# A Mamba scan on four engines: the table of slots in which TensorE, ScalarE and GpSimd do the side work, rewritten

## The reference, cut to what matters

```python
mu = seq.mean(-1, keepdims=True)
var = ((seq - mu) ** 2).mean(-1, keepdims=True)
h = (seq - mu) * jax.lax.rsqrt(var + EPS) * ln_g + ln_b
xz = h @ in_w
xs, z = jnp.split(xz, 2, axis=-1)             # 192 + 192 channels
xc = silu(depthwise causal conv of xs, 4 taps, + conv_b)
dbl = xc @ xproj_w
dt, Bm, Cm = split(dbl)                        # 6, 16, 16
delta = jax.nn.softplus(dt @ dt_w + dt_b)
dA = jnp.exp(delta[..., None] * A)             # 192 channels x 16 states
dBx = delta[..., None] * Bm[:, :, None, :] * xc[..., None]
hstates = scan: h_t = dA_t * h_(t-1) + dBx_t
y = jnp.einsum('blds,bls->bld', hstates, Cm) + Dp * xc
y = y * jax.nn.silu(z)
return seq + y @ out_w
```

## Time and profile before

| what | value |
|---|---|
| median of 3 runs | 7506.49 us |
| the profiled execution's own time | 7508.82 us |
| its span in the trace | 7506.7 us |
| TensorE, matmul busy | 6068.7 us (81%) |
| VectorE busy | 6432.9 us (86%) |
| ScalarE busy | 5446.9 us (73%) |
| GpSimd busy | 5465.7 us (73%) |
| Mamba phase | from 0 to about 2844 us |

### The profile page before, as it was taken

One profiled execution on the slowest core, in us unless ns is written; L12 is line 12 of the kernel. 1 busy time (PEld: TensorE's weight loads), 2 busy tenths in 40 slices (PEclk: granted clock), 3 DMA queues, 4 the chain that ended last, 5 costly groups with the idle time before them and its releaser, 6 DMA issues. The chain is left out here.

```text
span 7506.7 us, 105881 instructions
## 1 busy us (share of the span) xinstructions
PE 6068.7 (81%) x18336; PEld 2113.4 (28%) x18336; DVE 6432.9 (86%) x7490; ACT 5446.9 (73%) x11128; POOL 5465.7 (73%) x4289
## 2 busy tenths in 40 slices
PE   7888888888888872888888888888887768798696
PEld 2222222222222220222222222222222113498252
DVE  6999999999999995499999999999999985533636
ACT  7888888888888873577777778777777764322757
POOL 5888888888888881488898898888888871000606
PEclk8999999889989986888999999999999888997898
DMA  4445445445445445587888888888877773346222
GB/s 101 108 104 117 107 106 116 107 108 115 106 106 116 106 101 143 115 186 182 186 187 185 187 189 186 185 188 187 187 183 186 184 165 92 124 137 195 81 57 77
DMA packets 584349, 1050.60 MB, mean 140 GB/s; under 512 B 105735, under 2 KB 140732, under 8 KB 579100
## 3 DMA queue, kind: packets, MB, share of 16 engines
q1 hardware_dynamic: 584060, 1047.70, 58.7%
HBM read 857.89 MB, written 189.54 MB: 140 GB/s over the span
## 5 line engine op out<-in xcount | busy, mean ns | idle before, releaser
L1644 POOL TENSOR_TENSOR scan_prod<-scan_hs,scan_BC_rep 128x512 f32<-128x512 f32 x1536 | 1943.8, 1273 | 312.8 <-DVE scan_hs L1568 303.8
L664 POOL TENSOR_TENSOR mamba_prod<-mamba_hs,mamba_BC_rep 128x512 f32<-128x512 f32 x1536 | 1919.7, 1274 | 216.6 <-DVE mamba_hs L621 214.8
L621 DVE TENSOR_TENSOR_SCAN mamba_hs<-mamba_dA,mamba_carry,mamba_dbx 128x512 f32<-128x512 f32 x1152 | 1425.3, 1265 | 1.6
L1193 PE MATMUL scan_u_rep<-scan_du,scan_sel 96*128 96x512 f32 x1536 | 935.2, 693 | 538.7 <-DVE scan_hs L1568 538.5
L546 ACT ACTIVATE mamba_dA<-mamba_delta_rep,mamba_a_neg 128x512 f32<-128x512 f32 x1536 | 1092.5, 712 | 121.5 <-DVE mamba_hs L621 118.8
L1418 ACT ACTIVATE scan_dA<-scan_delta_rep,scan_a_neg 128x512 f32<-128x512 f32 x1536 | 1092.3, 712 | 96.1 <-DVE scan_hs L1568 84.7
L1568 DVE TENSOR_TENSOR_SCAN scan_hs<-scan_dA,scan_carry,scan_dbx_even 128x512 f32<-128x512 f32 x768 | 975.8, 1271 | 45.6 <-ACT scan_carry L1398 27.9
L1568 DVE TENSOR_TENSOR_SCAN scan_hs<-scan_dA,scan_carry,scan_u_rep 128x512 f32<-128x512 f32 x768 | 976.3, 1271 | 40.8 <-ACT scan_carry L1398 36.7
L600 DVE TENSOR_TENSOR mamba_dbx<-mamba_u_rep,mamba_BC_rep 128x512 f32<-128x512 f32 x1152 | 776.7, 674 | 88.1 <-PE mamba_u_rep L332 75.6
L1967 POOL TENSOR_TENSOR ffn_sq<-ffn_xm 96x512 f32<-96x512 f32 x64 | 66.3, 1036 | 954.4 <-DVE ffn_xm L1935 943.3
L332 PE MATMUL mamba_u_rep<-mamba_du,mamba_sel 96*128 96x512 f32 x768 | 466.5, 692 | 317.4 <-DVE mamba_hs L621 316.9
(11 more groups left out here) (286 smaller groups left out, 10776.8 us busy)
## 6 DMA issues: line engine op xcount, KB each, us to landing
scan_BC_rep<-proj_rows SPq DMA_DIRECT2D x1024, 256.0 KB, 6.4
scan_delta_rep<-proj_rows SPq DMA_DIRECT2D x1024, 192.0 KB, 3.6
mamba_BC_rep<-bc_units SPq DMA_DIRECT2D x512, 256.0 KB, 8.1
mamba_delta_rep<-delta_units SPq DMA_DIRECT2D x512, 192.0 KB, 3.7
proj_rows<-scan_dbc SPq DMA_DIRECT2D x256, 224.0 KB, 3.4
delta_units<-mamba_delta SPq DMA_DIRECT2D x128, 192.0 KB, 5.8
by_n<-fin_res SPq DMA_DIRECT2D x32, 768.0 KB, 3.2
fmid_src<-by_n SPq DMA_DIRECT2D x32, 768.0 KB, 5.2
```

The lines of the kernel that those rows point to most:

```text
L621: nc.vector.tensor_tensor_scan(hs[:, s % RING_H], dA[:, s % RING_A], dbx_bank(s)[:], carry[:, bass.ds(at, 1)], op0=ALU.mult, op1=ALU.add). ...
L664: pool.tensor_tensor(prod[:, (G * u + s) % RING_P], hs[:, s % RING_H], BC_rep[:, u, QUADS + s % QUADS], ALU.mult).then_inc(s_prod, 1)
L1193: nc.tensor.matmul(u_rep[c][:], sel[:, c], du[:, k], start=True, stop=True).then_inc(s_rep_u, 1)
L1644: pool.tensor_tensor(prod[:, (G * k + s) % RING_P], hs[:, (G * k + s) % RING_H], BC_rep[:, k, 2 + s % 2], ALU.mult).then_inc(s_prod, 1)
```

## The change

Only the numbers of slots change, and with them the order of instructions on TensorE, ScalarE and GpSimd. VectorE's and SyncE's code stays as it is. No instruction is added or taken away from a slot's work. (The changed file is three lines shorter, so its line numbers are 1 to 3 lower.)

TensorE, `next_step`, `ahead_step` and the output product:

```diff
-                if s == 0:
+                if s == 1:
                     project_z(lay, m, 1)
-                elif s == 3:
-                    project(lay, m, v, 0)
-                elif s == 5:
-                    project(lay, m, v, 1)
+                elif s == 4:
+                    for half in range(2):
+                        project(lay, m, v, half)
...
-                if s == 8:
+                if s == 10:
                     mean(m, v)
-                elif s == 10:
+                elif s == 12:
                     var(m, v)
...
-                    if s == 9 and prev is not None:
+                    if s == 7 and prev is not None:
                         project_out(prev, n - 1, 1 - u, 0)
                         project_out(prev, n - 1, 1 - u, 1)
```

ScalarE:

```diff
-                if s in (3, 4, 6):
-                    to_raw(lay, m, {3: 1, 4: 2, 6: 3}[s])
-                elif s == 5:
+                if s in (4, 7, 8):
+                    to_raw(lay, m, {4: 1, 7: 2, 8: 3}[s])
+                elif s == 6:
                     silu_x(m, v)
-                elif s == 9:
+                elif s == 12:
                     softplus_begin(lay, m, 0)
                     softplus_end(m, 0)
-                elif s == 11:
+                elif s == 14:
                     copy_bc(m)
                     softplus_begin(lay, m, 1)
-                elif s == 12:
                     softplus_end(m, 1)
-                elif s == 14:
                     silu_z(m, v)
```

More of the change, by code:

```diff
@@ L507, in next_step @@
             def next_step(s, lay, m, v):
-                if s in (3, 4, 6):
-                    to_raw(lay, m, {3: 1, 4: 2, 6: 3}[s])
-                elif s == 5:
+                if s in (4, 7, 8):
+                    to_raw(lay, m, {4: 1, 7: 2, 8: 3}[s])
+                elif s == 6:
                     silu_x(m, v)
-                elif s == 9:
+                elif s == 12:
                     softplus_begin(lay, m, 0)
                     softplus_end(m, 0)
-                elif s == 11:
+                elif s == 14:
                     copy_bc(m)
                     softplus_begin(lay, m, 1)
-                elif s == 12:
                     softplus_end(m, 1)
-                elif s == 14:
                     silu_z(m, v)
             def ahead_step(s, lay, m):
-                if s == 13:
+                if s == 15:
                     square(m)
-                elif s == 16:
+                elif s == 17:
                     rsqrt(m)
@@ L529, in ahead_step @@
                     affine(lay, m)
-                elif s == 23:
+                elif s == 22:
                     to_raw(lay, m, 0)
@@ L555, in body @@
                         next_step(s, nxt, n + 1, 1 - u)
-                    if s == 10 and prev is not None:
+                    if s == 8 and prev is not None:
                         evict_y(n - 1, 1)
-                    if s == 20:
+                    if s == 19:
                         evict_y(n, 0)
-                    if s == 15 and prev is not None:
+                    if s == 19 and prev is not None:
                         evict_out(n - 1)
@@ L665, in body @@
                                        ALU.mult).then_inc(s_prod, 1)
-                    if s == 6 and prev is not None:
+                    if s == 5 and prev is not None:
                         gate(n - 1, 1 - u, 1)
-                    if s == 18:
+                    if s == 20:
                         gate(n, u, 0)
@@ L675, in ahead_step @@
             def ahead_step(s, m):
-                if s == 12:
+                if s == 14:
                     normalise(m)
             def next_step(s, m, v):
-                if s == 5:
+                if s == 8:
                     add_softplus(m, v, 0)
-                elif s == 8:
+                elif s == 12:
                     add_softplus(m, v, 1)
-                elif s == 9:
+                elif s == 15:
                     input_times_delta(m, v)
```

## The result

The changed kernel takes 7539.44 us (median of 6 runs, 7536.70 to 7542.45) against 7504.63 us for the kernel before (6 runs, 7494.86 to 7511.48). The ratio is 1.0047, with an interval of 1.0034 to 1.0059: **slower by 35 us** where I had forecast 26 us faster (7480 against 7506.49). The profiled execution took 7542.45 us with a span of 7540.3, 33.6 us more than before.

What follows compares the result with a forecast made beforehand. VectorE, 98.5% busy in the Mamba phase, was taken as the bound, with 26.8 us of waits for TensorE to gain. 7508.8 - 29.9 + 3.2 = 7482.1, less 2.3 for the profiled run, gave 7480 us, range 7470 to 7500.

Steps and rivals of the forecast that it cites:

- SyncE: DMA-issuing queue, same code: B and C go some 3 us later, later transfers wanted only next unit; cost nothing.
- second kind of waits: VectorE's 24 waits, 12.4 us, put down to its own scans where the two-unit loop body starts again; left as is.
- TensorE, slots 7 to 12: Mamba units: slot 11's `rep_input` starts early enough, margin 1.1 to 3.8 us; gain 29.9 us, bounds 0 and 29.9.
- 34 waits: VectorE's waits for TensorE's `rep_input` before the `dbx` of group 16, 26.8 us in all; claimed to go.
- TensorE, slots 0 to 4: Mamba units: both projections in slot 4 start at the same moment as before, the last z product later; nothing.
- ScalarE, slot 14: Mamba units: eight instructions in one piece take 6.84 us; `dA` of slot 15 ready with margin 2.4 us; nothing.
- GpSimd: Mamba units: `du` moves to slot 15 behind `normalise`, ends at 32.6 us into the unit, wanted at 34.9; nothing.
- Prologue: Before the units: projection starts about 1.2 us later and 2.02 us of `var` stand bare; cost 3.2 us, bounds 0 and 6.
- Sum: Whole kernel: 7508.8 - 29.9 + 3.2 = 7482.1, predicted as 7480 us, 0.35% less.
- The third: Rival: VectorE waits for `du` or spreads of B and C at a unit's group 0; 0.5 us each, 7511; chance 0.06.
- The first: Rival: ScalarE too late with `dA` for scan 15, 3.0 us in some 62 units, 7666 us; chance 0.10.
- The second: Rival: TensorE still late in slot 11, half the waits at group 16 come back, 7495 us; chance 0.14.

Runs made afterwards that it cites:

- burst at 26: Changed kernel with SyncE holding the unit's second burst of transfers until scan 1 of the next unit is done; 7488.11 us, ratio 0.9967 to the kernel before.

## Why the prediction was wrong

**The step that failed** is SyncE: "Its code is the same but what it waits for shifts [...] Nothing." It is tied to the sentence on the second kind of waits, "No edit touches VectorE's code, so I leave it as it is." I had the shift right. It gave the store of `delta` half 0 at about T0 + 18 (18.0 in unit 19 after) and B and C some 3 us later than T0 + 19.0 (21.9). Then I asked only whether the data would be there when it is wanted, and for the later transfers wrote "wanted in the next unit". That holds: no wait for a DMA appeared. But I didn't lay out the second burst, and didn't ask what else uses the DMA engines at T0 + 42. In SyncE's order the store of `delta` half 1 stands behind the reads of B and C (issued at 912.65 before, 931.76 after), and the burst waits about 10 us until that store has landed (941.86 - 931.76 = 10.1 after, 922.96 - 912.65 = 10.3 before). So it shifts with B and C, from T0 + 32.1 to 37.1, and its transfers last to about T0 + 43. The 24 waits at the turn were listed, and I took their 0.5 us for a fixed price. By the runs that price isn't fixed: it depends on what the DMA engines are doing at the turn. This term was +54 us where I had put 0, and taken out (burst at 26) it leaves 7488.

**The other steps, in the order of the text.**

- *TensorE, slots 7 to 12*: right. `copy_bc` starts at T0 + 16.5 (16.6 laid out), `mean` at 18.4 (18.4 laid out), the `rep_input` of slot 11 at 21.3 (21.2 at full clock), `var` at 25.1 (about 25.0). All 34 waits went. TensorE's granted clock from 66 to 2830 us rose from 0.90 to 0.93.
- *TensorE, slots 0 to 4*: right, ScalarE's 63 waits for the first projection (153.2 us) are gone.
- *ScalarE, slot 14*: right. From `copy_bc` at 921.22 to the `dA` of slot 15 at 927.96 the block takes 6.74 us (6.84), and VectorE never waits for `dA`. Each table load is followed by its ACTIVATE after 1.30 us. With 2.66 us per switch, the rule of the Trainium skill (ScalarE: Activation LUTs, What ACT_TABLE_LOAD costs), the block would by my estimate have been about 9.5 us; this case's trace doesn't agree with that rule, and the measurement decides.

```profile
921.22 0.59 ACT L487 ACTIVATE mamba_bc<-mamba_pre 32x512 f32<-32x512 f32 x1
...
924.29 1.28 ACT L465 ACT_TABLE_LOAD   x1
925.59 1.06 ACT L465 ACTIVATE mamba_xz<-mamba_raw 96x1024 f32<-96x1024 f32 x1
926.66 1.28 ACT L466 ACT_TABLE_LOAD   x1
927.96 0.72 ACT L543 ACTIVATE mamba_dA<-mamba_delta_rep,mamba_a_neg 128x512 f32<-128x512 f32 x1
```

- *GpSimd*: right. `xh` starts at T0 + 27.7 (27.7), and `du` ends at 32.6 (32.6).
- *Prologue*: mechanism right, size just over its upper bound: +6.3 against 3.2, bounds 0 and 6. The projection started 1.1 us later (1.2), but took 7.04 us instead of 5.37 at a lower clock:

```profile
36.55 7.04 PE L317 MATMUL mamba_pre<-mamba_xz,mamba_w_proj 96*96 96x512 f32 x8 [3.26 <-ACT mamba_raw L453]
```

  The granted clock of that stretch, 36 to 44 us, is 0.57, and was 0.72 over 35 to 41 us before. It isn't the same in each run: with the burst at 26, whose prologue is the same code, the same eight products took 5.34 us and the first `dbx` was at 69.72, +3.8. So in part this size was bad luck.
- *Sum*: with the turns as they were, the forecast was 7480 from a kernel at 7506.49, 0.35% less; measured with the burst at 26, 0.33% less. "First `dbx` near 69 us and last scan near 2807": that kernel has 69.7 and 2806.4.

**The rivals.** The third had the right kind of cause, "another queue becomes the wait", and the wrong place: it looked for data that comes late at group 0, and it was code at the turn. Its price, 0.5 us in each unit (31 us), was below what came, 2.2 us more at each of 24 turns (54 us), and its chance of 0.06 was small for a queue whose shift of 3 us I had worked out myself. The first came true only where TensorE's slots move alone. The second did only where ScalarE's and GpSimd's do.

**What stays open.** A turn without a burst waits 0.5 us because VectorE goes on 2.0 us behind the middle packet and that packet comes 1.5 us ahead. But what decides the moment of the middle packet could not be seen: the trace shows when it moved, not when it was asked for, and the first of the three comes 4 us ahead of this turn in either kernel. Nor does a run tell whether the burst holds the packet up in the DMA engines, as theory A has it, or elsewhere on its way. That the packets are VectorE's code is read from the middle one's fixed distance to VectorE's last scan (1.3 to 1.6 us ahead at every turn without a burst); the trace doesn't name the engine. A burst held only so far that it ends before the turn, or its transfers issued from another queue, wasn't tried.

## What to carry to other kernels

A reordering of compute that leaves the DMA code untouched still moves every transfer that waits on that compute; lay those out on the same time axis, and ask not only when the data is wanted but what else the DMA engines must carry in those microseconds. At the point where a loop body starts again that was code: here an idle time under "issue" (or put to the engine's own last instruction) that returned once per turn hung on the branch and on the packets of code, its price was not fixed, and a burst on it made 0.5 us into 2.8. If the code can be afforded, write the loop out; if not, keep bursts clear of the turn, which one semaphore wait on the issuing queue did here: VectorE's waits at the turns went from 66.2 to 12.8 us.

## What the runs showed of the hardware

- The wait at a loop's turn grows with data transfers in flight: 12.8 us over 24 turns with the burst behind them, 64.8 us with the burst on them, 0 without a branch. At each of the 24 turns VectorE goes on 2.0 to 2.3 us behind one packet of code, and it is this packet that the burst makes late.
- The labels of a wait aren't its cause. The same 24 waits are put to "DVE mamba_hs" when short, to "issue" when long, and up to four of them to TensorE.
- Two groups of instructions moved together gain (23 us with the burst at 26, 15 us with the loops written out); each moved alone loses, 50 us and 177 us.
- Writing out the loops of one phase is worth 29 us to the kernel before (7516.37 to 7487.28), about half of it at the turns. The changed one went from 7539.44 to 7472.64 in different batches, 67 us. More code has to come in: over the whole run queue 14 brings 210 packets of mostly 8 KB against 225, but queue 8 brings 103 of 16 KB against 64.
